# Two global attentions: row maxima transposed twelve pieces later, and a zero-weight matmul in front of every pair of score matmuls

## The reference

```
x = layernorm(x + causal attention, 16 heads of 16, 4 key/value heads)
x = layernorm(x + mixture of 8 experts, top 2)
x = layernorm(x + attention, 16 heads of 16, masked by pages of 64 tokens)
x = layernorm(x + 2 layers of (local attention + gated unit))
```

## Time and profile before

| | us |
|---|---|
| runs of the kernel before | 5850.08, 5887.48, 5936.67 (median 5887.48) |
| profiled execution, its own time | 5825.77 |
| its span from first to last instruction | 5824.2 |
| PE busy | 4707.0 (81%) |
| PEld busy | 3020.7 (52%) |
| DVE busy | 3059.5 (53%) |
| ACT busy | 2344.9 (40%) |
| POOL busy | 861.0 (15%) |
| mean granted TensorE clock | 0.851 of full speed |

### The profile page before, as it was taken

The page is one execution under the profiler, slowest core; times in us unless marked ns, Lnnn a source line. Parts: engine busy times, 40 slices in busy tenths (PEclk is TensorE's granted clock), DMA queues, the critical chain, the costliest instruction groups (busy, mean ns, idle before and its releaser), DMA issues. The chain is left out here.

```text
span 5824.2 us, 81282 instructions
## 1 busy us (share of the span) xinstructions
PE 4707.0 (81%) x25828; PEld 3020.7 (52%) x25828; DVE 3059.5 (53%) x5338; ACT 2344.9 (40%) x3695; POOL 861.0 (15%) x1228
## 2 busy tenths in 40 slices
PE   4999999952999993759999998476997967699787
PEld 2444434341887882323434343355775755577566
DVE  1777767632344442746667674475443547444354
ACT  1365555521344441204555555133443423334333
POOL 1011211115000004010111110132111003211100
PEclk8698889875999996856778898698998989899888
DMA  7111221023112112350333220334332123333211
GB/s 213 25 27 27 35 40 29 11 96 114 48 47 75 46 44 85 130 103 9 49 47 50 38 40 22 120 118 133 111 118 78 33 60 118 125 118 110 73 43 33
DMA packets 271929, 413.90 MB, mean 71 GB/s; under 512 B 40836, under 2 KB 178945, under 8 KB 268028
## 3 DMA queue, kind: packets, MB, share of 16 engines
q0 software_dynamic: 64160, 224.28, 16.3%
q1 hardware_dynamic: 202844, 181.40, 9.7%
q10 hardware_dynamic: 4608, 4.20, 0.2%
HBM read 252.70 MB, written 156.19 MB: 70 GB/s over the span
## 5 line engine op out<-in xcount | busy, mean ns | idle before, releaser
L509 DVE TENSOR_REDUCE G_mpart<-G_pm 128x1 f32<-128x512 f32 (+3 forms) x1152 | 705.1, 656 | 340.3 <-PE G_pm L419 331.0
L509 DVE TENSOR_REDUCE B_mpart<-B_pm 128x1 f32<-128x512 f32 (+3 forms) x1152 | 704.4, 656 | 300.0 <-PE B_pm L419 290.4
L495 ACT ACTIVATE G_p<-G_psc 128x1024 f32<-128x1024 f32 (+3 forms) x640 | 544.1, 894 | 470.5 <-PE G_psc L458 469.7
L495 ACT ACTIVATE B_p<-B_psc 128x1024 f32<-128x1024 f32 (+3 forms) x640 | 543.1, 894 | 445.2 <-PE B_psc L458 444.6
L419 PE MATMUL G_pm<-G_ks,G_qs 48*128 48x512 f32 (+3 forms) x1280 | 523.5, 521 | 8.9 <-DVE G_mpart L509 4.3
L419 PE MATMUL B_pm<-B_ks,B_qs 48*128 48x512 f32 (+3 forms) x1280 | 510.3, 507 | 9.4 <-DVE B_mpart L509 4.1
L458 PE MATMUL G_psc<-G_qs,G_ks 50*128 50x512 f32 (+3 forms) x1280 | 357.9, 453 | 16.0 <-issue 13.4
L419 PEld LDWEIGHTS G_pm<-G_ks,G_qs 48*128 48x128 f32 x1280 | 231.4, 224 | 265.1 <-DVE G_mpart L509 171.4
L435 PE MATMUL G_po<-G_p,G_v 128*32 128x512 f32 (+3 forms) x2560 | 359.4, 639 | 6.7 <-DVE G_o L523 6.0
L419 PEld LDWEIGHTS B_pm<-B_ks,B_qs 48*128 48x128 f32 x1280 | 226.2, 218 | 259.3 <-DVE B_mpart L509 175.0
L458 PE MATMUL B_psc<-B_qs,B_ks 50*128 50x512 f32 (+3 forms) x1280 | 347.3, 440 | 10.0 <-issue 7.4
(11 more groups left out here) (308 smaller groups left out, 7879.6 us busy)
## 6 DMA issues: line engine op xcount, KB each, us to landing
J_v<-lve POOLq DMA_DIRECT2D x64, 520.0 KB, 4.2
J_k<-lkT POOLq DMA_DIRECT2D x64, 512.0 KB, 5.1
lve<-I_v SPq DMA_DIRECT2D x64, 260.0 KB, 2.1
lqT<-I_tT SPq DMA_DIRECT2D x64, 256.0 KB, 2.4
lkT<-I_tT SPq DMA_DIRECT2D x64, 256.0 KB, 2.6
J_q<-lqT POOLq DMA_DIRECT2D x64, 256.0 KB, 4.2
ein<-Z_z SPq DMA_DIRECT2D x8, 1228.0 KB
E_xin<-ein POOLq DMA_DIRECT2D x8, 1152.0 KB, 6.4
```

Of the source, the lines that this page charges most:

```text
L495: act.activation(p[:, t % 2, 2 * pr:2 * pr + 2, off:CH], psc[:, 2 * pr:2 * pr + 2, off:CH], ACT.Exp, scale=SC).then_inc(e_done[pr], 1)
L509: dve.tensor_reduce(mpart[:, heads[0] % 2, a:a + len(heads), qb, kc], pm[slots[e]][:, 0:len(heads) * w].rearrange("p (h k) -> p h k", k=w) ...
```

## The change

Two edits inside `attention`, so both count for both attentions.

The turn of a chunk stands 12 pieces behind the chunk's last piece in the list of events instead of 4. The fold stays where it was.

PE gets a new instruction, `keep_busy`, in front of the wait for each pair of scores: a bf16 matmul with a 128x128 block of zeros as weights and four copies of the identity (512 columns) as the moving operand, added to `po`. It is left out in the steps with kb = 1, and in the very first step of the attention. The zeros are set once by DVE, and PE waits for that at the start.

```diff
-        for behind, kind in ((1, "fold"), (4, "turn")):
+        for behind, kind in ((1, "fold"), (12, "turn")):
...
+        zero = sb("zero", [P, P], BF16)
...
+            def keep_busy(i, t):
+
+                if steps[t][1] == 1 or static(i, 0) and t == 0:
+                    return
+                pe.matmul(po[:], zero[:], idb[:].unsqueeze(1).to_broadcast([P, GRP, P]), start=False, stop=False,
+                          skip_group_check=True)
...
                     for pr in range(2):
+                        keep_busy(i, t)
                         pe.wait_ge(e_done[pr], i * NS + t + 1)
...
             pe.wait_ge(c_in, 16 * CONSTS)
+            pe.wait_ge(ready, 2)
             pe.wait_ge(q_in[0], 16 * LOADS)
...
             dve.memset(m[:].bitcast(F32), 0.0)
+            dve.memset(zero[:], 0.0)
             dve.memset(one[:], 1.0).then_inc(ready, 1)
```

## The result

The changed kernel takes 6910.6 us (median of 5 runs, 6888 to 7126) against 5890.3 for the kernel before: a ratio of 1.1805, 95% interval 1.1734 to 1.1875. That is 1,020 us slower; 143 were forecast, and the range ended at 6235. The profiled execution is the slowest of the five (7126.2 us, mean clock 0.742; the others have 0.764 to 0.774), so its clock losses are some 200 us larger than those of the median.

The account below looks back on a forecast made before the run. PE was taken to pace both attentions. Zero matmuls +351, clock -187 and turn waits -21 gave +143 us, so 5887.5 + 143 = 6030 us, 2.4% slower; range 5795 to 6235.

Parts of the forecast that it names:

- The bound: In both attentions PE sets the pace, busy 937 of 981 us in the first; DVE and ACT wait for it.
- rival C: At the score matmuls PE already waits, so zeros cost little and the kernel is faster, 5632 to 5796 us; chance 0.14.
- The price of one zero matmul: Before each score pair, 0.33 us each at full clock; 1,064 counted, +351 us.
- The last steps: At each attention's end ACT is the bound, so the 42 zero matmuls there were counted at 0.
- The turn: Moving each chunk's turn eight pieces later removes PE's waits for POOL in both attentions: -21 us.
- the rows of maxima: After the moved turn these rows still reach PE in time, with 9 us left: priced at 0.
- The clock: In both attentions after the openings, full clock returns for 8 tenths of 657 us at half clock: -187 us.
- rival D: In the attentions the zeros' price is paid and the clock does not come back: 6218 to 6284 us; chance 0.14.
- The "above" bound of the price: At most 0.49 us for each zero matmul, since one over all rows must drain both halves of the array.
- The 0.8 of 234 us: Share expected back of the 234 us that full clock in both attentions after the openings could give: 187 us.
- Rival A: The forecast itself: PE pays for the zeros, the attentions' clock mostly returns, 110 to 317 us more; chance 0.47.

Follow-up runs that it names:

- the other place: The changed kernel with both zero matmuls of a step together just in front of the weighing instead of before each score pair: 5943 us.

## Why the prediction was wrong, point by point

- *The bound.* Right. PE paces both attentions, and the zero matmuls were hardly ever covered: PE waits 0.4 us for an exponential at the scores of the first attention, and rival C (the gap in front of the scores is real) has nothing for it.
- *The price of one zero matmul*, 0.33 us. The distance to the next load was right, 0.32 at full clock and 0.54 at half. What was wrong was to let the lost overlap and PE's idle time cancel: the overlap was lost and nothing came back, 0.39 each by the estimate over a whole iteration and 0.42 by three stretches at full clock. The last steps did not hide theirs either, which the forecast had counted at 0: from the last turn to the last scores the changed kernel takes 42.8 us at full clock in both attentions, with 35 zero matmuls in it, and the moved turn alone 34.9 us in its second attention, with 3.4 of them at half clock. Over all 1,148 the term is +454 us at full clock where +351 was forecast, inside the bound of 0.49.
- *The turn*, -21 us, and 0 for the rows of maxima. The waits for POOL went, but the term at 0 was wrong: with the turn alone moved, PE waits 27.2 us in the second attention, six times. Nine us were thought enough for a copy and two small DMAs; at 2788 they took 26, and that the DMA engines might be full then was not considered. Beside the clock this is small, and in the changed kernel it nearly vanishes (4.5 us), since its steps are so much longer.
- ***The clock*, -187 us. This is the step that failed.** It came out at +834 in the profiled execution and some +570 at the medians. I had read the earlier trace rows as cause and effect, an idle microsecond and then half clock, and concluded that filling PE would raise the clock. The row that spoke against it I had used for rival D only: in the opening PE is busy 52 of 54 us at 0.50. The "above" bound of the price was the same fact seen once, and priced once: draining both halves of the rows was taken as 0.16 us of time, and what such places do to the clock was not asked. The 0.8 of 234 us had no row behind it.
- *Rival D* named the right sign (nothing comes back) but no mechanism by which the clock could fall below the kernel before, so its 6284 is still 600 us short.
- *A slip.* Rival A gives its upper end as 317 us and works it out as 313. Nothing else uses it.

What the runs show: a matmul over all rows in front of each pair of half-height score matmuls, twice a step, leaves the clock at half for most of both attentions while PE is busy all the time, and at half clock each zero matmul costs 0.54 instead of 0.32. Shown by: the turn left in its place or other data, no change; fewer columns at the same place, no better; one such matmul a step, nearly no fall; half the rows or another place, cured; no added work but other pairs, a smaller fall. Most of these are single runs, but the differences between 5859 or 5943 and 7188 us are far outside the spread.

Not shown is why the clock falls. That fewer half-height matmuls run at once is not it, since their share is the same 65% at 0.58 and at 0.96. A candidate is the weight loads that wait for the matmul before them: 0.32 us from the zeros' load to the next, and longer stretches at full clock both in the changed kernel and with the other pairs. No run separates it from other causes.

The Trainium skill, "TensorE: Matmul & The Clock Gate", section "Why this matters for your kernels", says that a TensorE kept continuously busy gets to full clock. This case disagrees: the opening, mostly half-height matmuls, is busy for 52 of 54 us at 0.50, and the changed kernel for 1682 of 1694 us at a mean of 0.58. The same page's Part 3, on packing small matmuls, says that a weight load overlaps a running matmul only when their row groups differ. Here the traces agree in part. Between the zeros and the scores there is no such overlap: 0.32 us from load to load. But in the kernel with the other place the loads of the two zero matmuls, both over all rows, pass within 0.11 us (905.79, x2) while the two matmuls take 0.53, so there the second load did not wait for the first matmul to end.

## What to carry to other kernels

Before adding work to PE "for the clock", look for what runs side by side there: a matmul over all rows between half-height ones costs its own time, their overlap, and possibly the clock, and the last may be the largest by far. If a filler is wanted, try it next to an operation that takes all rows already (0.23 us each here, against 0.42 between the half-height ones) and with 512 columns, not 128, and expect it to cost about what it brings. A small DMA that was far ahead of its use can become late by a move of two steps; look at what else the DMA engines do at that time. When two kernels' clocks are compared, see that their profiled runs are alike: runs of the kernel before alone lie between mean clocks of 0.820 and 0.852. And take a stretch where the engine is busy at half clock, such as the opening here, as proof against any forecast that being busy is enough.

## What the hardware did that I had not expected

- PE busy for 534 of 535 us in one piece at half clock (224 to 759 us of the changed kernel), while a sparser PE (937 of 981 us) had 0.85.
- An order of the same instructions moves the clock: pairing heads 0 and 2 instead of 0 and 1 took it to 0.72 in the first attention, and over the whole run from 0.835 to 0.811.
- The same matmul of 512 columns at the same place costs 0.42 us over 128 rows and 0.07 over 64.
- Two DMAs of 8 KB took 26 us from issue to use while the DMA engines were full.
- Fewer streamed columns, lower clock: at the first place 0.58 with 512 columns and 0.50 with 128, beside the weighing 0.96 and 0.80.
- Zeros, an identity or dense numbers make no difference to the clock that can be seen: 0.58 to 0.71 in the first attention, 0.61 to 0.64 in the second.
